# Block 0 of a fused attention and expert layer: row maxima from 64 rows per head, router products in another bank, first score passes ahead of the maxima

## What is computed

```python
xn = layernorm(x)                                  # (2048, 128)
q, k, v = xn @ Wq, xn @ Wk, xn @ Wv                # 16 heads of 64
attn = softmax(q @ k.T * 64 ** -0.5)               # per head, 2048 x 2048
a = (attn @ v) @ Wo + bo
e = argmax(softmax(xn @ router_w.T))               # one of 8 experts per token
f = relu(xn @ expert_fc[e]) ** 2 @ expert_proj[e]
out = x + a + f
```

## Time and profile before

| | |
|---|---|
| median of three runs | 1391.95 us (1389.67 to 1391.98) |
| the profiled execution | 1392.0 us, of which 1390.3 us are the span from its first to its last instruction |
| PE busy | 1366.4 us, 98% of the span |
| POOL, DVE, ACT busy | 1120.9, 1077.7, 735.8 us |
| mean granted clock of PE | 0.991 of full speed |

### The profile page before, as it was taken

One profiled execution on the slowest core, in us unless ns is written; L12 is line 12 of the kernel. 1 busy time (PEld: TensorE's weight loads), 2 busy tenths in 40 slices (PEclk: granted clock), 3 DMA queues, 4 the chain that ended last, 5 costly groups with the idle time before them and its releaser, 6 DMA issues.

```text
span 1390.3 us, 20003 instructions
## 1 busy us (share of the span) xinstructions
PE 1366.4 (98%) x6447; PEld 869.9 (63%) x6447; DVE 1077.7 (78%) x1468; ACT 735.8 (53%) x1318; POOL 1120.9 (81%) x908
## 2 busy tenths in 40 slices
PE   6999999999999999999999999999999999999997
PEld 4665566576665666666766666656667566666644
DVE  7888887777776867777678777778777786788877
ACT  5354465464564554545545546546456455556543
POOL 7679997787887877877778777778777787789995
PEclk9799999999999999999999999999999999999999
DMA  3242112321132201322013311133111231111000
GB/s 86 67 105 54 37 43 64 75 58 30 43 72 67 68 19 42 84 64 59 20 42 94 69 44 42 40 74 84 30 42 45 64 89 25 25 23 33 11 19 23
DMA packets 65095, 72.12 MB, mean 52 GB/s; under 512 B 8992, under 2 KB 38240, under 8 KB 64992
## 3 DMA queue, kind: packets, MB, share of 16 engines
q1 hardware_dynamic: 63968, 68.75, 20.2%
q0 software_dynamic: 1024, 2.10, 0.5%
HBM read 17.83 MB, written 5.11 MB: 17 GB/s over the span
## 4 chain that ended last, share of the span: by engine, by line
PE 93%; DVE 2%; DMA 1%; POOL 1%; SPq 1%; issue 1%; ACT 1%; POOLq 0%; DVEq 0%; ACTq 0%
PE OB L1101 31%; PE SB L1057 17%; PE MB L1079 16%; PE SB L1061 16%; PE XB L1138 2%; PE XB L1129 2%; PE XB L1147 2%; PE XB L1046 1%; PE XB L1039 1%; POOL acc L498 1%; SPq L366 1%; DMA K<-low 1%; PE XB L1108 1%; PE XB L1110 1%; PE XB L1109 1%
## 5 line engine op out<-in xcount | busy, mean ns | idle before, releaser
L498 POOL TENSOR_TENSOR acc<-acc,ex 128x512 f32<-128x512 f32 x717 | 914.8, 1301 | 100.2 <-DVE acc L788 41.7
L765 DVE TENSOR_REDUCE mx<-MB 128x1 f32<-128x512 f32 x992 | 656.2, 688 | 229.8 <-PE MB L1079 224.9
L612 ACT ACTIVATE ex<-SB 128x512 f32<-128x512 f32 x1024 | 606.7, 598 | 331.6 <-PE SB L1061 268.0
L1101 PE MATMUL OB<-ex,V 128*64 128x512 f32 x2048 | 452.7, 594 | 0.0
L1057 PE MATMUL SB<-Q,K 128*128 128x512 f32 x1024 | 422.9, 413 | 1.1 <-ACT ex L612 1.1
L1061 PE MATMUL SB<-Q,K 128*128 128x512 f32 x1024 | 400.6, 391 | 1.2 <-DMA Q<-mrow 1.2
L1079 PE MATMUL MB<-K,Q 128*128 128x512 f32 x992 | 390.1, 395 | 0.4
L1101 PEld LDWEIGHTS OB<-ex,V 128*64 128x64 f32 x2048 | 143.9, 137 | 284.3 <-issue 273.0
L1057 PEld LDWEIGHTS SB<-Q,K 128*128 128x128 f32 x1024 | 193.1, 189 | 97.3 <-issue 53.5
L788 DVE TENSOR_TENSOR acc<-acc,ex 128x512 f32<-128x512 f32 x179 | 205.5, 1148 | 13.5 <-ACT ex L612 1.0
L1079 PEld LDWEIGHTS MB<-K,Q 128*128 128x128 f32 x992 | 187.6, 189 | 44.1 <-DVE mx L765 2.9
(11 more groups left out here) (142 smaller groups left out, 612.6 us busy)
## 6 DMA issues: line engine op xcount, KB each, us to landing
Q<-high SPq DMA_DIRECT2D x124, 128.0 KB, 2.3
K<-high SPq DMA_DIRECT2D x112, 128.0 KB, 2.3
Q<-low SPq DMA_DIRECT2D x64, 128.0 KB, 2.3
K<-low SPq DMA_DIRECT2D x56, 128.0 KB, 2.3
w<-fc SPq DMA_DIRECT2D x23, 256.0 KB, 2.7
w<-projT SPq DMA_DIRECT2D x23, 256.0 KB, 3.1
sorted_x<-res SPq DMA_DIRECT2D x1, 1472.0 KB, 6.9
tok<-sorted_x SPq DMA_DIRECT2D x23, 64.0 KB, 1.7
```

The source lines that it names most:

```text
L498: pool.tensor_tensor(a[:, :], src[:, :], EX[h][ex_slot(kt)][:, :], ALU.add).then_inc(done, 1)
L612: act.activation(EX[h][ex_slot(kt)][:, :], SB[bank_of(n, 2 * kt + h)][:, :], ACT.Exp).then_inc(a_e[h], 1)
L765: dve.tensor_reduce(mx[:, m % 2, u:u + 1], MB[bank_of(m, i)][:, :], AX.X, ALU.max).then_inc(v_m, 1)
L1101: mm = pe.matmul(OB[own[h], :], V[(n // JB) % 2][:, k, own[h]], EX[h][ex_slot(k)][:, :], start=(k == 0), stop=(k == NT - 1))
```

## The change

The opening of block 0 is arranged anew; the loops behind it stay as they are, but for the banks and waits shown.

- `max_pair` multiplies only the own 64 rows of each head, and a pair is now the same unit of the two heads. It needs no copied rows: the waits for `d_k0` and `d_q0` ahead of it are gone, and it waits for ACT's copies (`a_q`, `a_k0`) instead.
- The order on PE is new: q of block 0 starts before the second chunk is turned (`first_q`), k of chunks 0 and 1 come before the third chunk is turned, and the fourth chunk's turn and k of chunks 2 and 3 stand among the pairs. Chunks 2 and 3 are both turned into XB, so the fourth waits for ACT's copy of the third.
- BETWEEN has 12 entries in place of 9 and puts V's products, the router's and q of block 1 at other pairs. The router's products go to OB.
- ACT no longer copies Q1 to Q2 (`copy_q0`); SP does with two transfers more. `high_k0` is cut in two, and the copy to ex (`copy_k0`) comes later for chunks 0 and 1.
- `low_q0` on DVE moves behind the second pair.
- `place_max(0)` no longer waits for all of POOL's zeroing, and the rows of ones go in two parts (`place_ones`), of which the first comes early.
- Three first passes of score tiles (`FIRST_S`) come ahead of the wait for the copied maxima.

```diff
-        BETWEEN = {0: ("v", 0), 2: ("v", 1), 4: ("v", 2), 6: ("v", 3), 8: ("q", 1),
-                   9: ("r", 0), 11: ("r", 1), 13: ("r", 2), 15: ("r", 3)}
-        TX = [MB[0], MB[1], SB[0], SB[1]]
-        START_Q, START = MB[2], [OB, SB[2], MB[2], OB]
+        BETWEEN = {0: ("t", 3), 1: ("k", 2), 3: ("v", 0), 4: ("k", 3), 5: ("r", 0), 6: ("q", 1), 8: ("v", 1), 9: ("r", 1),
+                   11: ("v", 2), 12: ("r", 2), 13: ("r", 3), 14: ("v", 3)}
+        TX = [MB[0], MB[1], XB, XB]
+        START_Q, START = MB[2], [OB, SB[2], OB, SB[2]]
...
-        ORDER = [r * JB + c for c in range(JB) for r in range(2 * TB)]
+        FIRST_S = 3
...
                 def spread_q0():
+                    sp.wait_ge(a_q, 1)
+                    for h in range(2):
+                        copy(Q2[0][h][own[h], :], Q1[0][h][own[h], :], d_q0)
                     sp.wait_ge(v_q, 1)
...
+                    sp.wait_ge(g_i, 5)
+                    sp.wait_ge(g_z, 4)
+                    place_ones(0)
+                    spread_k0(0)
+                    spread_k0(1)
                     spread_q0()
-                    for c in range(JB):
-                        spread_k0(c)
+                    spread_k0(2)
                     load_w(Lin(1))
                     load_wo(Lin(0))
-                    sp.wait_ge(d_q0, 32)
-                    sp.wait_ge(a_q0, 1)
+                    spread_k0(3)
+                    sp.wait_ge(d_q0, 64)
                     sp.sem_inc(d_q[0], QD)
+                    spread_q(Lin(1))
...
                     high_q0()
                     high_k0(0)
+                    high_k0(1)
                     turned(2)
-                    high_k0(1)
-                    turned(3)
-                    high_k0(2)
-                    copy_q0()
-                    for u in range(UNITS // 2):
-                        if u == 5:
-                            high_k0(3)
...
+                    copy_k0(0)
+                    for p in range(UNITS // 2):
+                        kind, c = BETWEEN.get(p, (None, 0))
+                        if kind == "t":
+                            turned(c)
+                            copy_k0(1)
+                        elif kind == "k":
+                            high_k0(c)
+                            copy_k0(c)
...
                     rows(2)
-                    low_q0()
                     rows(3)
                     for p in range(UNITS // 2):
                         maxima_pair(p)
-                        if p in BETWEEN:
-                            kind, c = BETWEEN[p]
-                            if kind == "q":
-                                low_q(Lin(c))
+                        if p == 1:
+                            low_q0()
+                        kind, c = BETWEEN.get(p - 1, (None, 0))
+                        if kind == "q":
+                            low_q(Lin(c))
...
                 def max_pair(p):
 
+
+                    q, c = p % TB, p // TB
                     wait(pe, v_m, 2 * p - 2)
-                    for a in range(2):
-                        u = ORDER[2 * p + a]
-                        h, q, c = u // (TB * JB), u // JB % TB, u % JB
-                        mm = pe.matmul(PAIR[p % 2][:, a * QB:(a + 1) * QB], Q1[0][h][:, q * P:(q + 1) * P],
-                                       K1[0][h][:, c * QB:(c + 1) * QB], start=True, stop=True)
-                    mm.then_inc(t_m, 2)
+                    if p == 0:
+                        pe.wait_ge(a_x, 2)
+                        pe.wait_ge(a_q, 1)
+                    if q == 0:
+                        pe.wait_ge(a_k0, c + 1)
+                    for h in range(2):
+                        pe.matmul(PAIR[p % 2][:, h * QB:(h + 1) * QB], Q1[0][h][own[h], q * P:(q + 1) * P],
+                                  K1[0][h][own[h], c * QB:(c + 1) * QB], start=True, stop=True).then_inc(t_m, 1)
...
+                    def first_q():
+                        pe.wait_ge(v_w, 1)
+                        pe.wait_ge(a_x, 1)
+                        q = slice(0, QB)
+                        pe.matmul(START_Q[:, :], whi[0][:, 0, :], xhi[:, q], start=True, stop=False)
+                        pe.matmul(START_Q[:, :], wlo[0][:, 0, :], xhi[:, q], start=False, stop=False)
+                        turn_x(1)
+                        pe.wait_ge(g_lo, 1)
+                        pe.matmul(START_Q[:, :], whi[0][:, 0, :], xlo[:, q], start=False, stop=True).then_inc(t_q, 1)
+
                     turn_x(0)
-                    turn_x(1)
-                    pe.wait_ge(g_lo, 1)
-                    make_q(Lin(0), START_Q)
+                    first_q()
                     first_k(0)
+                    first_k(1)
                     turn_x(2)
-                    first_k(1)
-                    turn_x(3)
-                    first_k(2)
-                    pe.wait_ge(a_x, JB)
-                    pe.wait_ge(d_q0, 32)
                     for p in range(UNITS // 2):
-                        if p % TB == 0:
-                            pe.wait_ge(d_k0[p // TB], 32)
                         max_pair(p)
...
                     for u in range(EARLY, MIDDLE):
                         max_unit(Lin(1), u)
+                    for g in range(FIRST_S):
+                        high_scores(Lin(0), g // 2, g % 2)
```

More of the change, by code:

```diff
@@ L182, in layer @@
         sums = [[sem(f"sum{h}_{k}") for k in range(2)] for h in range(2)]
-        g_on, g_k0, a_k0, d_one = sem("g_on"), sem("g_k0"), sem("a_k0"), sem("d_one")
+        g_on, g_k0, a_k0 = sem("g_on"), sem("g_k0"), sem("a_k0")
+        d_one = [sem(f"d_one{k}") for k in range(2)]
         d_x, d_c = [sem(f"d_x{j}") for j in range(JB)], sem("d_c")
@@ L397, in spread_q0, with place_ones @@
                         copy(Q1[0][h][other[h], :], low[own[h], :], d_q0)
+                def place_ones(k):
+                    for h in range(2):
+                        sp.dma_start(K2[k][h][maxrow[h], :].bitcast(F32), ones[0:NT, :]).then_inc(d_one[k], 16)
                 def place_max(m):
@@ L401, in place_max @@
                     wait(sp, a_nm, m.times(1, 1))
-                    wait(sp, g_z, 4 + 2 * QS)
+                    wait(sp, g_z, 4 + 2 * QS if m.off else 4)
                     for h in range(2):
@@ L437, in first @@
                     sp.sem_inc(d_k[0], JB * KD)
-                    spread_q(Lin(1))
-                    sp.wait_ge(g_i, 5)
+                    place_max(Lin(0))
                     sp.wait_ge(g_z, 4 + 2 * QS)
[L441 to L444, removed]
+                    place_ones(1)
                 def one(n):
@@ L645, in max_rows @@
                         wait(act, d_nm[old % QS], (old // QS).times(32, 32))
-                    nm_bank = OB if m.off == 0 else XB
-                    act.activation(mrow[:, :], nm_bank[0:2 * TB, 0:P], ACT.Copy).then_inc(a_nm, 1)
+                    act.activation(mrow[:, :], XB[0:2 * TB, 0:P], ACT.Copy).then_inc(a_nm, 1)
                 def take_o(n):
@@ L684, in high_q0 @@
                     ins.then_inc(a_q, 1)
[L686 to L690, removed]
                 def copy_tokens(r):
@@ L1047, in expert_down, with high_scores @@
                     mm.then_inc(t_down, 1)
-                def scores(n, kt, h):
+                def high_scores(n, kt, h):
                     par, k, keys = (n // JB) % 2, n % QS, slice(kt * P, (kt + 1) * P)
-                    tile = SB[bank_of(n, 2 * kt + h)]
                     m, i = ring_before(n, 2 * kt + h)
@@ L1054, in scores, with low_scores @@
                         wait(pe, a_e[i % 2], m.times(NT, i // 2 + 1))
+                    elif bank_of(n, 2 * kt + h) == 2:
+                        pe.wait_ge(a_k, JB)
                     if kt == 0 and h == 0:
                         q_ready(pe, n)
-                    pe.matmul(tile[:, :], K1[par][h][:, keys], Q1[k][h][:, :], start=True, stop=False)
+                    pe.matmul(SB[bank_of(n, 2 * kt + h)][:, :], K1[par][h][:, keys], Q1[k][h][:, :], start=True, stop=False)
+                def low_scores(n, kt, h):
+                    par, k, keys = (n // JB) % 2, n % QS, slice(kt * P, (kt + 1) * P)
                     if kt == 0 and h == 0:
                         wait(pe, d_nm[k], (n // QS).times(32, 32))
-                        wait(pe, d_one, 64)
-                    pe.matmul(tile[:, :], K2[par][h][:, keys], Q2[k][h][:, :], start=False, stop=True).then_inc(t_s, 1)
+                        wait(pe, d_one[par], 32)
+                    pe.matmul(SB[bank_of(n, 2 * kt + h)][:, :], K2[par][h][:, keys], Q2[k][h][:, :],
+                              start=False, stop=True).then_inc(t_s, 1)
                 def max_unit(m, i, u=None):
@@ L1096, in times_v @@
                     if kt == 0:
+                        if n.off == 0:
+                            pe.wait_ge(v_mask, 1)
                         wait(pe, a_o, n.times(1))
@@ L1196, in first @@
+                        if kind == "t":
+                            turn_x(c)
```

(12 more changed lines are left out.)

57 lines of the change are left out of this document (21 added, 36 removed).

## The result

The changed kernel takes 1395.09 us (median of 8 runs, 1394.74 to 1396.53) against 1390.12 us for the one before in runs beside it (8 runs, 1387.35 to 1391.98). The ratio is 1.0037, 95% interval 1.0026 to 1.0048: slower by 0.37%, some 5 us. The forecast was 1385.8 us and faster.

A forecast was written before the change was run, and what follows sets the result against it. PE, 93% of the chain, was taken to run without a stop behind the opening. Gains of 4.5 by nm, 1.0 and 1.0 make 6.5 us, less 0.3 for the clock: 1392.0 - 6.2 = 1385.8, range 1384.0 to 1390.3.

The forecast's parts named there:

- case 1: Forecast: clock stays up from pair 2 to the units but for a short fall near 18 us; gain 6.2, chance 0.55.
- rival 2: Clock falls among block 0's pairs and PE becomes the bound; gain 1.5 to 4 us, middle 2.6, chance 0.30.
- case 2: Same as rival 2: clock falls among the pairs, 2.4 to 4.1 us go back; gain 1.5 to 4, chance 0.30.
- Rival 4: Pair halves run one behind the other with the clock down; end 4.5 us later than before, chance 0.05.
- PE's load at full clock: Among the pairs at 2.4 GHz, PE's pair of 0.45 us and its job stay hidden under DVE's 1.14 per pair.
- The opening: Up to the second pair: DVE reads the first at 16.5 us, not 21.18, and the second at 19.1.
- K<-K: Transfer on the chain ahead of the first pair; its 2.35 us were to leave the path.
- The hole at pair 8: V's second chunk takes XB only after `low_q(1)`, 29.15 us, so pair 9 comes 0.3 late.
- Behind nm: From nm to the fourth score tile: 1.0 us gained by nm's turn, 1.0 by passes already done and the clock.

The follow-up runs named there:

- e1: Changed kernel with six extra unread 512-column products in PE's hole at pair 8, ahead of V's second chunk: 1390.25 us, ratio to before 1.0007.
- e12: Changed kernel with four extra wide products behind pair 0 alone, the hole at pair 8 left open: 1395.40 us, ratio to before 1.0037.
- e11: Changed kernel with six extra wide products in the hole at pair 8 and four behind pair 0: 1388.44 us, ratio to before 0.9987.
- e6: Changed kernel with DVE's low part of block 1's q one pair earlier: 1390.80 us, ratio to before 1.0001.
- e3: Changed kernel with the router's products 64 columns wide in place of 8: 1395.96 us, ratio to before 1.0031.
- e4: Kernel before with six extra unread 512-column products in its own hole, ahead of its first router products: 1389.35 us, ratio to before 0.9993.
- e13: e11 with DVE's low part of block 1's q one pair earlier and four extra products in place of six: 1388.77 us, ratio to before 0.9987.

## Why the prediction was wrong

**The step that failed** is case 1, "the clock stays up from pair 2 to the units", and with it the claim that DVE is the bound there. The clock fell in the stretch from 31 to 32 and was back in that from 45 to 46, and from pair 9 to pair 15 PE took 13.5 us where DVE's six distances are 6.8. Of the 9.3 us between the forecast (1385.8) and the median, 8.2 are there when nm is done (47.04 for 38.8). The forecast's start from 1392.0, where the median of before is 1390.1, hid another 1.9. The mechanism was named as rival 2 with a chance of 0.30, and the Trainium skill (TensorE: Matmul & The Clock Gate, A second HAM failure mode) speaks of a swing between the two clocks in an engine that idles briefly; the trace after shows one such fall, half clock from 32 to 45 us. I gave 0.55 to the clock staying up, from a gap of 1.3 us that cost nothing; the hole that did cost was 1.53. By e1 against the changed kernel, and e12 against e11, filling this one hole is worth 4.8 and 7.0 us; e6, which makes it shorter and adds no product, gives 4.3.

**The size of case 2 was wrong too**, gain 1.5 to 4 where 5 were lost. From pair 10 on I counted 9.2 us of PE: six pairs at 0.43, two router jobs, two of V. The profile after has 13.5 there. The router job right behind pair 9 was left out, 1.8. A pair took 0.72 and not 0.43 (one of the six, next to another pair, did take 0.43), as the changes of shape, priced at full clock alone, are dearer at half clock: 1.5 in all. Router and V jobs took 1.80 and 2.00, not 1.51 and 1.78: 0.6 and 0.4. That makes 4.3, the whole difference.

**Rival 4**, slower with a chance of 0.05, had the sign right by luck. Its mark, a pair over 0.65 us at half clock, was met with 0.72. Its mechanism was not: halves one behind the other would take 0.86, and a pair behind a pair took 0.43.

**PE's load at full clock** was the other step. "DVE's 1.14 covers them" compares a pair and a job, 0.45 + 1.06, with 1.14, and is wrong as it stands. e11, whose clock is up in this stretch, has 7.8 us from pair 9 (31.65) to pair 15 (39.45) where six distances of DVE are 6.8, and DVE waits for PE at pairs 9, 10, 14 and 15. So nm was to be done at 38.8, and with the clock held it is at 40.9; 1.0 of the 2.1 us arises in this stretch, 0.8 between the second pair and pair 9, and 0.3 ahead of them.

**The opening.** The first pair came at 17.88 and not 16.5. PE could start k of chunk 1 only at 14.50, when POOL's xlo was there, and did it and the third chunk's turn at half clock, so it came to pair 0 at 16.93. In e3 and e11, where the clock had risen by then, the first pair is read at 16.59. The second came at 19.83, forecast 19.1, bound by what was named: ACT's copies of chunk 2 and PE's turn of chunk 3. K<-K did leave the path. The hole at pair 8 was seen, but priced as 0.3 us of DVE and not by what it does to the clock.

**Behind nm** the distances were right: 3.2 us to the second pass (3.1 forecast), 6.8 to the fourth tile (6.95). That is 2.2 us less than before (53.80 - 47.04 against 52.29 - 43.31), but a part of it is the clock, which was down there in the profile of before and up in that of after. With the clock down for 3.4 us of it e11 takes 6.8, and e4, which has the old order, takes 8.0 with the clock down for 5.9 and the kernel before 9.0 with it down throughout. How the 2.2 divide between order and clock is not shown. Not seen was wlo, 1.35 us and not 0.41, just as POOL begins its sums at 53.71; PE waits 0.76 for it. e11 has 0.41 at the same place in its list: there DVE starts at 47.84 and POOL's sums only at 48.05; in e1 and e13 it is 1.34 and 1.36.

**The whole, with the clock held up to nm** (in e11's profile it is down from the stretch 43 to 44 to that from 47 to 48): e11 is 0.13% faster than before (interval 0.04 to 0.21), 2.5 us and not 6.2. Its profiled execution is 5.3 faster in span than that of before, but it is the earliest of e11's, and that of before among the latest of its own. The forecast took one profiled execution for the typical one: later runs of before had medians of 1390.7 to 1391.2, from 1387.35 to 1395.07. The spread of before goes with its mean clock: its executions at 0.997 take 1387.35 to 1389.40 us, those at 0.991 take 1390.96 to 1393.35. The profiled one had 0.991, so the forecast started from an execution that had itself lost time to the clock.

## What to carry to other kernels

An opening made shorter by sparing PE its work can lose more than it gains: before PE is given holes, count what the next 10 us would cost at half clock, with every job and every change of shape, and fill the holes with products that nobody reads if the count is larger. An idle wait off the chain of DVE is then not free. And where runs of one kernel spread by more than the change is worth, look in the lengths of the matmuls for where the clock rose and fell in each profile, and trust the mean clock only where that shows the same: it orders the executions of the kernel before, and misses the late rise of e6.

## What the hardware showed that I had not expected

- PEclk is 1.00 ahead of the first recorded fall even where matmuls run at half clock: e6 at 36.43 has eight router products in 1.80 us (0.99 at full clock) under a PEclk of 1.00, and a mean clock of 0.997 at 1399.51 us, one of the highest means of all and one of the longest times.
- Two products of 64 rows in different halves of the array follow the next two after 0.34 us at full clock (pairs 2 and 3 of the changed kernel), against 0.46 for two of 128 rows: they overlap only in part. With the changes of shape beside other jobs it is 0.43, and nothing is gained.
- The same subtraction of 128x256 on DVE took 0.41 us where it began 0.21 us ahead of POOL's addition (e11) and 1.35 where POOL had begun 0.22 us sooner (the changed kernel).
